# Router rows of layer 0 turned behind the next batch's queries, into a buffer of their own

## Chip, cores and metric

One core of a Trainium2 chip runs the whole program. Its engines are TensorE (PE, with its weight loads as PEld), VectorE (DVE), ScalarE (ACT) and GpSimd (POOL), each with a queue of its own that runs in order; SyncE (SP) issues most transfers. The metric is the device time of one execution in microseconds.

## What is computed

Four batches of 512 rows of width 256 pass through two layers. Cut to the steps in question:

```
x = x + tanh(g) * MLP(attention(layernorm(x), ctx))      # layer 0, 16 heads, 64 context rows
n = layernorm(x)
logits = n @ router_w + router_b                          # 8 experts
x = x + tanh(g) * max_prob * expert[argmax](n)            # one expert per row
x = x + tanh(g) * attention(layernorm(x), ctx)            # layer 1
x = x + tanh(g) * ternary_ffn(layernorm(x))
```

## The kernel before, in words

The order of work on each engine is written out by hand, with semaphores between the engines. No scheduler has a part in it. Layer 0 runs in four batches (0 to 3) of four tiles of 128 rows. The function `attention(l, b, first_batch, last_batch)` exists once for each engine and holds that engine's share of batch `b`. It is software-pipelined: while the attention of batch `b` runs, the normalised rows of batch `b+1` are turned and multiplied to queries, and the router's work for batch `b-1` is done, whose rows were finished at the end of the batch before.

TensorE does this in a batch of layer 0: `turn(0)`, scores of tile 2, `turn(1)`, scores of tile 3 (`turn` transposes the probabilities of one tile into the two PSUM banks `t_bank`, L740; `scores` is L724); then `router_turn(b-1)` (L881), eight transposes of the rows that VectorE's second layer norm wrote (`xn2`, printed as `ew`), which wait for `ln["rt"]["xn"]`; then `values(0)` (L758), between whose halves stand `router_products(b-1)` (L888, sixteen recorded products of 8 columns), the small `weight_sum` (L857) and `turn_rows(b+1)` (L696); then `queries(b+1)` (L711) in two halves, of which the second overwrites a bank in which `weight_sum` and the router left results, and so waits for VectorE's `w_mean` (L1512) and logits (L1534); then `turn(2)`, scores of the next batch's tile 0, `turn(3)`, `values(1)`, and the products of the MLP (L812, then L827).

ScalarE copies what is turned out of `t_bank` to SBUF: `turned` (L1167) for the probabilities, `router_rows` (L1142) for the router's rows, `turned_rows` (L1127) for the query rows. The last two write the same buffer, `xn_t`. Its order in a batch is turned(0), turned(1), router_rows, exponentials of tile 2 (L1137), output (L1172), turned_rows, output, exponentials of tile 3, the two copies of the queries (L1132), turned(2), turned(3). The first half of the queries also waits until VectorE has read the bank that it overwrites (`o_lo`, L1560).

VectorE's order is: scores of tile 2 (maximum L1476, difference L1481), a pass over the ternary weights (L1530), sums of tile 2 (L1490, L1493), `o_lo`, scores of tile 3, `o_lo`, `w_mean`, logits, statistics (L1414), sums of tile 3, scores of the next batch's tile 0, the layer norm of the batch after (`xn`, L1436), two more `o_lo`, sums of tile 0, and so on. GpSimd multiplies the probabilities by the reciprocals (L506), and adds the bias rows (L474).

In batch 3 there are no queries; `ternary_chunk` (L874, copied by L1147) is there in their place, in three pairs around turn(2) and turn(3).

## Time and profile before

| what | value |
|---|---|
| median of 3 runs | 603.48 us (597.16 to 603.55) |
| profiled execution, its time | 595.08 us |
| its span | 592.7 us |
| PE, PEld busy | 499.5 us (84%), 364.4 us (61%) |
| DVE, ACT, POOL busy | 419.2, 294.2, 247.1 us |
| mean granted clock of TensorE | 0.927 of full speed |

The numbers below the medians come from the one profiled execution. Busy time says how much an engine has to do, not what ends last. Within layer 0 that is read from the timeline: the bracket behind a row says how long the engine stood idle before it and which instruction released it. Batch 1 of layer 0 begins with the transposes at 63.09 us, batch 2 at 99.97 and batch 3 at 138.73; the expert stage follows at about 200 us.

### The profile page before, as it was taken

The numbers are of one execution on the slowest core, as the hardware profiler recorded it, in microseconds if no ns is written. First come the engines' busy times: TensorE is split into PE (matmuls) and PEld (weight loads), VectorE is DVE, ScalarE is ACT, GpSimd is POOL, SyncE is SP. The second block draws the span as 40 slices with busy tenths as digits, with TensorE's granted clock in tenths as the row PEclk, the third lists the DMA queues.
The fourth block names the chain that finished last, engine by engine and source line by source line (L and its number), as shares of the span: only waits on it lengthen the run. The fifth ranks groups of instructions, "written<-read, shape, count | busy, mean of one in ns | idle before, by whom it ended". The sixth has DMA issues, their size and how long they took to land.

```text
span 592.7 us, 10230 instructions
## 1 busy us (share of the span) xinstructions
PE 499.5 (84%) x3061; PEld 364.4 (61%) x3069; DVE 419.2 (71%) x809; ACT 294.2 (50%) x521; POOL 247.1 (42%) x314
## 2 busy tenths in 40 slices
PE   7888899896998699899999999944897777649994
PEld 3456658566784278788888888812553544425562
DVE  6598898787546987494756823227979899588992
ACT  1446555362654466483755623203454444427884
POOL 5454263344300311020212110066367878538996
PEclk9989899699698899899999999979599989588999
DMA  7940100100167156555554310022000000000112
GB/s 212 296 147 1 37 0 2 36 0 1 35 215 236 31 161 221 180 178 168 174 178 154 94 35 18 18 81 71 0 1 1 1 1 1 0 0 2 36 35 71
DMA packets 35162, 46.40 MB, mean 78 GB/s; under 512 B 2764, under 2 KB 25304, under 8 KB 35128
## 3 DMA queue, kind: packets, MB, share of 16 engines
q1 hardware_dynamic: 30856, 39.02, 20.4%
q0 software_dynamic: 1680, 4.59, 2.7%
q10 hardware_dynamic: 2592, 2.36, 1.2%
q8 instruction: 18, 0.29, 0.2%
q14 instruction: 16, 0.13, 0.1%
HBM read 38.36 MB, written 7.60 MB: 78 GB/s over the span
## 4 chain that ended last, share of the span: by engine, by line
PE 45%; DVE 28%; POOL 10%; issue 7%; ACT 3%; DMA 2%; SPq 2%; DVEq 1%; POOLq 0%; ACTq 0%
PE s_tile L976 16%; PE bank L997 8%; DVE s_max L1476 4%; DVE p_sum L1490 4%; PE bank L827 3%; DVE probs L1481 3%; PE bank L986 3%; DVE stats L1414 2%; DVE xn L1436 2%; DVE ew L1436 2%; PE bank L711 2%; PE s_tile L1070 2%; POOL probs_t L614 2%; DMA w<-in_L_xattn_W 2%; DVE ew_lo L1746 2%
## 5 line engine op out<-in xcount | busy, mean ns | idle before, releaser
L506 POOL TENSOR_TENSOR probs<-probs,p_rcp 128x1024 f32<-128x1024 f32 x32 | 60.9, 1907 | 94.3 <-DVE p_rcp L1493 94.3
L740 PE MATMUL bank<-ident,probs 128*128 128x128 f32 x256 | 40.4, 309 | 27.0 <-POOL probs L506 25.3
L976 PE MATMUL s_tile<-ew_hi,xs_hi 128*128 128x512 f32 x144 | 59.9, 416 | 3.7 <-DVE ew_lo L1746 2.5
L1167 ACT COPY probs_t<-bank 128x512 f32<-128x512 f32 x64 | 35.0, 588 | 47.1 <-PE bank L740 46.7
L976 PE MATMUL s_tile<-ew_hi,xs_lo 128*128 128x512 f32 x144 | 57.5, 399 | 0.0
L976 PE MATMUL s_tile<-ew_lo,xs_hi 128*128 128x512 f32 x144 | 57.4, 398 | 0.0
L740 PEld LDWEIGHTS bank<-ident,probs 128*128 128x128 f32 x256 | 32.9, 159 | 39.5 <-POOL probs L506 30.1
L564 POOL TENSOR_TENSOR token_now<-token_of,carried 128x1 uint32<-128x1 uint32 x17 | 3.8, 226 | 124.1 <-PE bank L960 124.1
L1764 DVE TENSOR_TENSOR probs_t<-s_tile,probs_t 128x512 f32<-128x512 f32 x36 | 24.8, 689 | 43.1 <-PE s_tile L976 41.7
L1137 ACT ACTIVATE probs<-probs 128x1024 f32<-128x1024 f32 x32 | 33.9, 1058 | 33.8 <-DVE probs L1481 33.7
L1476 DVE TENSOR_REDUCE s_max<-s_tile 128x16 f32<-128x1024 f32 x32 | 38.4, 1199 | 16.6 <-PE s_tile L724 16.5
L1746 DVE TENSOR_TENSOR ew_lo<-ew,ew_hi 128x512 fp32r<-128x512 f32 x64 | 40.4, 686 | 10.3 <-ACT ew_hi L1254 9.4
L1490 DVE TENSOR_REDUCE p_sum<-probs 128x16 f32<-128x1024 f32 x32 | 38.7, 1209 | 6.4 <-ACT probs L1137 6.3
L724 PE MATMUL s_tile<-k_bd,q_t 64*128 64x256 f32 x256 | 40.6, 433 | 3.0 <-ACT q_t L1132 3.0
L997 PE MATMUL bank<-ew_hi,act_hi 128*128 x144 | 42.2, 293 | 0.0
L1481 DVE TENSOR_TENSOR probs<-s_tile,s_max 128x1024 f32<-128x1024 f32 x32 | 39.2, 1225 | 2.0 <-DVE s_max L1476 0.3
L997 PE MATMUL bank<-ew_lo,act_hi 128*128 x144 | 40.5, 282 | 0.0
L997 PE MATMUL bank<-ew_hi,act_lo 128*128 x144 | 40.3, 280 | 0.0
L1254 ACT CAST ew_hi<-ew 128x512 fp32r<-128x512 f32 x64 | 35.5, 619 | 7.5 <-issue 7.5
L1768 DVE TENSOR_TENSOR act_lo<-bank,act_hi 128x512 fp32r<-128x512 f32 x36 | 24.8, 689 | 18.6 <-ACT act_hi L1295 18.6
L1295 ACT CAST act_hi<-bank 128x512 fp32r<-128x512 f32 x36 | 21.2, 588 | 30.4 <-PE bank L986 30.4
L1285 ACT ACTIVATE probs_t<-s_tile 128x512 f32<-128x512 f32 x36 | 21.5, 599 | 28.3 <-PE s_tile L976 24.6
(228 smaller groups left out, 1318.8 us busy)
## 6 DMA issues: line engine op xcount, KB each, us to landing
ew<-in_L_ffn_w SPq DMA_DIRECT2D x32, 512.0 KB, 5.0
ew<-in_L_ffn_w SPq DMA_DIRECT2D x8, 1024.0 KB, 5.7
slots_y<-xn ACTq DMA_DIRECT2D x18, 128.0 KB, 3.9
x_res<-in_x SPq DMA_DIRECT2D x4, 512.0 KB, 6.4
token_rows<-ew SPq DMA_DIRECT2D x4, 512.0 KB, 3.1
out_rows<-x_res SPq DMA_DIRECT2D x3, 512.0 KB, 3.0
w<-in_L_xattn_W SPq DMA_DIRECT2D x2, 512.0 KB, 9.4
ew<-in_L_ffn_w_gate SPq DMA_DIRECT2D x1, 1024.0 KB, 12.9
```

Of the source, the lines that this page charges most:

```text
L506: nc.gpsimd.tensor_tensor(p, p, p_rcp[:, i, :].unsqueeze(2).to_broadcast([P, H, M]), ALU.mult).then_inc(s["p_norm"], 1)
L724: last = nc.tensor.matmul(s_bank[i % 2][g][:, GH * M * m:GH * M * m + GH * M], q_t[rows, m, P * i:P * i + P], flat(k_bd[rows, m, bass.ds(n ...
L740: last = nc.tensor.transpose(t_bank[c][:, P * j:P * j + P], probs[:, i % 2, at:at + P], ident[:])
L976: last = nc.tensor.matmul(o[:], x, w, start=(k == 0 and n == 0), stop=(k == DK - 1 and n == 2))
L997: last = nc.tensor.matmul(y_bank[:, D * par:D * par + D], u, w, start=(c == 0 and n == 0), stop=(c == EK - 1 and n == 2))
L1137: nc.scalar.activation(probs[:, i % 2, :], probs[:, i % 2, :], ACT.Exp).then_inc(att[l]["a_exp"], 1)
L1167: last = nc.scalar.copy(flat(probs_t[:, i % 2, 4 * c:4 * c + 4, :]), t_bank[c][:])
L1254: last = nc.scalar.copy(hi, w)
L1476: nc.vector.tensor_reduce(s_max[:, i, :], s_tile[i % 2][:].rearrange("p (h s) -> p h s", h=H), AX, ALU.max).then_inc(s["v_max"], 1)
L1481: nc.vector.tensor_tensor(probs[:, i % 2, :].rearrange("p (h s) -> p h s", h=H), s_tile[i % 2][:].rearrange("p (h s) -> p h s", h=H), s_ma ...
L1490: nc.vector.tensor_reduce(p_sum[:, i, :], probs[:, i % 2, :].rearrange("p (h s) -> p h s", h=H), AX, ALU.add).then_inc(s["v_sum"], 1)
L1746: last = nc.vector.tensor_tensor(lo, w, hi.bitcast(F32), ALU.subtract)
```

## The change

The router's rows of batch `b-1` get a buffer of their own, `xr_t`, laid over the values of layer 1 (`v_blk1`, idle until layer 1's values are written; VectorE clears it again in the last batch, 128x1024). With it ScalarE's copies need not share `xn_t`. TensorE no longer turns the router's rows before `values(0)` but after `queries(b+1)`; scores of the next batch's tile 0 come before `turn(2)` instead of behind it; `turn(2)` now waits for ScalarE's two router copies (`r_e`), and the router's products stand between `turn(2)` and `turn(3)`. VectorE's logits move behind the next batch's scores of tile 0 and ahead of its layer norm. Its differences of tile 0 wait for `turn(2)`. The wait for the logits moves from the second half of the queries to the second half of `values(1)`. Layer 0's batch 0, all of layer 1 and the router's work for batch 3 keep their order.

```diff
+        xr_t = v_blk1[:].rearrange("p b j a -> p (b j a)")[:, 0:DK * N].rearrange("p (k n) -> p k n", k=DK)
 # TensorE, queries:
                     if l == 0 and m == 1 and not start:
                         pe.wait_ge(v_wm, n)
-                        if not first:
-                            pe.wait_ge(r_lg, n - 1)
 # TensorE, values:
+                        if half and k and l == 0 and not first_batch:
+                            pe.wait_ge(r_lg, b)
 # TensorE, between():
-                    if l == 0 and not first_batch:
-                        router_products(b - 1)
 # TensorE, attention:
                 scores(l, b, 3)
-                pe.wait_ge(s["a_pt"], TB * b + 2)
-                if l == 0 and not first_batch:
-                    router_turn(b - 1)
                 values(0)
                 if not last_batch:
                     queries(l, b + 1, first_batch, False)
...
+                if l == 0 and not first_batch:
+                    pe.wait_ge(s["a_pt"], TB * b + 2)
+                    router_turn(b - 1)
+                    if not last_batch:
+                        scores(l, b + 1, 0)
+                    pe.wait_ge(r_e, DK * b)
                 turn(2)
...
-                if not last_batch:
+                if not last_batch and (l == 1 or first_batch):
                     scores(l, b + 1, 0)
+                if l == 0 and not first_batch:
+                    if last_batch:
+                        pe.wait_ge(v_olo, 2 * DK * b + DK)
+                    router_products(b - 1, xr_t)
                 turn(3)
 # ScalarE, attention:
                 turned(1)
-                if l == 0 and not first_batch:
-                    router_rows(b - 1)
                 exps(l, b, 2)
                 output(0, 0)
                 if not last_batch:
-                    if l == 0 and not first_batch:
-                        act.wait_ge(r_l, b)
                     turned_rows(l, b + 1)
...
+                if l == 0 and not first_batch:
+                    if not last_batch:
+                        act.wait_ge(r_l, b - 1)
+                    router_rows(b - 1, xr_t)
                 turned(2)
 # VectorE, scores:
-                if i >= 2:
+                if i >= 2 or follows:
                     dve.wait_ge(s["t_pt"], 2 * g - 2)
 # VectorE, attention:
-                if l == 0 and not first_batch:
-                    router_logits(b - 1)
                 if not last_batch:
                     row_stats(phase, TB * b + 2 * TB)
...
-                    scores(l, b + 1, 0)
+                    scores(l, b + 1, 0, True)
                     if l == 0:
+                        if not first_batch:
+                            router_logits(b - 1)
                         dve.wait_ge(s["t_xt"], DK * b + 2 * DK)
                         norm_apply(phase, b + 3, TB * b + 2 * TB, xn)
+                if l == 0 and last_batch:
+                    router_logits(b - 1)
+                    nc.vector.memset(v_blk1[:], 0.0)
```

TensorE in batch 1, from the scores of tile 3 to `turn(3)`. Before:

```order
L724 MATMUL s_tile<-k_bd,q_t 128x256 x4
L881 MATMUL bank<-ident,ew 128x128 x8
L758 MATMUL bank<-probs_t,v_blk 32x256 x4
L888 MATMUL bank<-rw,xn_t 128x8 x8
L857 MATMUL bank<-w_sum,ones 128x1
L696 MATMUL bank<-ident,xn 128x128 x8
L758 MATMUL bank<-probs_t,v_blk 32x256 x4
L711 MATMUL bank<-xn_t,wq 128x512 x4
L740 MATMUL bank<-ident,probs 128x128 x8
L724 MATMUL s_tile<-k_bd,q_t 128x256 x4
L740 MATMUL bank<-ident,probs 128x128 x8
```

and changed (line numbers shift by one to five; `v_blk` is where the router's rows now lie):

```order
L723 MATMUL s_tile<-k_bd,q_t 128x256 x4
L759 MATMUL bank<-probs_t,v_blk 32x256 x4
L862 MATMUL bank<-w_sum,ones 128x1
L697 MATMUL bank<-ident,xn 128x128 x8
L759 MATMUL bank<-probs_t,v_blk 32x256 x4
L710 MATMUL bank<-xn_t,wq 128x512 x4
L886 MATMUL bank<-ident,ew 128x128 x8
L723 MATMUL s_tile<-k_bd,q_t 128x256 x4
L739 MATMUL bank<-ident,probs 128x128 x8
L893 MATMUL bank<-rw,v_blk 128x8 x8
L739 MATMUL bank<-ident,probs 128x128 x8
```

The router's transposes moved behind the queries, the next batch's scores ahead of `turn(2)`, and the router's products from ahead of the queries to directly before `turn(3)`.

TensorE in batch 3, from the scores of tile 3 to the last weight transposes. Before:

```order
L724 MATMUL s_tile<-k_bd,q_t 128x256 x4
L881 MATMUL bank<-ident,ew 128x128 x8
L758 MATMUL bank<-probs_t,v_blk 32x256 x4
L888 MATMUL bank<-rw,xn_t 128x8 x8
L758 MATMUL bank<-probs_t,v_blk 32x256 x4
L874 MATMUL s_tile<-ident_b,ew 128x128 x16
L740 MATMUL bank<-ident,probs 128x128 x8
L874 MATMUL s_tile<-ident_b,ew 128x128 x16
L740 MATMUL bank<-ident,probs 128x128 x8
L874 MATMUL s_tile<-ident_b,ew 128x128 x16
```

and changed:

```order
L723 MATMUL s_tile<-k_bd,q_t 128x256 x4
L759 MATMUL bank<-probs_t,v_blk 32x256 x8
L879 MATMUL s_tile<-ident_b,ew 128x128 x16
L886 MATMUL bank<-ident,ew 128x128 x8
L739 MATMUL bank<-ident,probs 128x128 x8
L879 MATMUL s_tile<-ident_b,ew 128x128 x16
L893 MATMUL bank<-rw,v_blk 128x8 x8
L739 MATMUL bank<-ident,probs 128x128 x8
L879 MATMUL s_tile<-ident_b,ew 128x128 x16
```

The router's transposes now stand between the first weight transposes (the L874, now L879, rows) and `turn(2)`, the products between the second ones and `turn(3)`.

VectorE in batches 1 and 2, around the logits (`w_mean` is the ternary scale, ISA and REGISTER_ALU rows are waits and addresses). Before:

```order
L1560 TENSOR_TENSOR o_lo<-bank,o_hi 128x256
L1511 REGISTER_ALU
L1512 REGISTER_ALU
L1512 TENSOR_SCALAR w_mean<-bank 128x1
L1515 REGISTER_ALU
L1515 RECIPROCAL w_inv<-w_mean 128x1
L1534 ISA
L1534 TENSOR_TENSOR logits<-bank,rb 128x32
L1414 ISA
L1414 BN_STATS stats<-x_res 128x6
```

and changed:

```order
L1480 ISA
L1481 TENSOR_REDUCE s_max<-s_tile 128x16
L1485 ISA
L1486 TENSOR_TENSOR probs<-s_tile,s_max 128x1024
L1539 ISA
L1539 TENSOR_TENSOR logits<-bank,rb 128x32
L1607 ISA
L1441 TENSOR_SCALAR xn<-x_res,mv,rstd 128x256 x4
L1565 TENSOR_TENSOR o_lo<-bank,o_hi 128x256 x2
```

The logits (L1539, before L1534) stood ahead of the statistics; they now stand between the differences and the layer norm `xn`, and wait there for the products.

## Rows read from the trace of the kernel before

**Rows 1.** Table of stretches: start:end, length, busy us (count) of PE, PEld, DVE, ACT, POOL, granted clock, DMA

```profile
69.70:80.30 10.60, 10.37 (x58) 6.40 (x59) 10.10 (x17) 5.45 (x9) 3.77 (x2) 0.85 0.15 51
106.60:120.10 13.50, 13.44 (x58) 8.98 (x59) 10.95 (x18) 5.68 (x9) 3.77 (x2) 0.62 0.12 40
147.30:163.20 15.90, 14.39 (x120) 11.30 (x120) 9.29 (x12) 10.00 (x15) 5.63 (x3) 0.68 0.10 34
```

**Rows 2.** Timeline, TensorE, batch 1: start, duration, line, operation, count, [idle before, releaser]

```profile
69.76 1.94 PE L881 MATMUL bank<-ident,ew 128*128 128x128 f32 x8 [2.42 <-DVE ew L1436]
...
72.64 2.06 PE L888 MATMUL bank<-rw,xn_t 128*128 128x8 f32 x16
...
76.58 3.95 PE L711 MATMUL bank<-xn_t,wq 128*128 128x512 f32 x8 [0.16 <-ACT xn_t L1127]
80.37 1.04 PE L740 MATMUL bank<-ident,probs 128*128 128x128 f32 x8
81.33 1.14 PE L724 MATMUL s_tile<-k_bd,q_t 64*128 64x256 f32 x8
83.28 1.09 PE L740 MATMUL bank<-ident,probs 128*128 128x128 f32 x8 [0.81 <-POOL probs L506]
```

**Rows 3.** Timeline, TensorE's weight loads, batch 1, second half of the queries

```profile
78.55 0.30 PEld L711 LDWEIGHTS bank<-xn_t,wq 128*128 128x128 f32 x2 [0.81 <-DVE w_mean L1512]
```

**Rows 4.** Timeline, VectorE, batch 1

```profile
74.74 0.37 DVE L1560 TENSOR_TENSOR o_lo<-bank,o_hi 128x256 fp32r<-128x256 f32 x1
...
77.85 0.15 DVE L1512 TENSOR_SCALAR w_mean<-bank 128x1 f32 x1
...
78.28 0.19 DVE L1534 TENSOR_TENSOR logits<-bank,rb 128x32 f32 x1
...
82.52 1.22 DVE L1476 TENSOR_REDUCE s_max<-s_tile 128x16 f32<-128x1024 f32 x1 [0.98 <-PE s_tile L724]
...
84.92 3.01 DVE L1436 TENSOR_SCALAR xn<-x_res,mv,rstd 128x256 f32 x4
...
88.50 1.21 DVE L1490 TENSOR_REDUCE p_sum<-probs 128x16 f32<-128x1024 f32 x1
```

**Rows 5.** Timeline, ScalarE, batch 1

```profile
72.22 1.06 ACT L1137 ACTIVATE probs<-probs 128x1024 f32<-128x1024 f32 x1
...
75.45 1.07 ACT L1127 COPY xn_t<-bank 128x512 f32<-128x512 f32 x2 [1.91 <-PE bank L696]
...
80.57 0.69 ACT L1132 ACTIVATE q_t<-bank,bq_s 128x512 f32<-128x512 f32 x1 [1.28 <-PE bank L711]
...
86.50 1.06 ACT L1137 ACTIVATE probs<-probs 128x1024 f32<-128x1024 f32 x1
```

**Rows 6.** Timeline, TensorE, batch 2

```profile
106.66 1.60 PE L881 MATMUL bank<-ident,ew 128*128 128x128 f32 x8 [2.45 <-DVE ew L1436]
...
109.20 3.58 PE L888 MATMUL bank<-rw,xn_t 128*128 128x8 f32 x16
...
122.27 1.09 PE L740 MATMUL bank<-ident,probs 128*128 128x128 f32 x8
```

**Rows 7.** Timeline, VectorE, batch 2

```profile
116.50 0.42 DVE L1560 TENSOR_TENSOR o_lo<-bank,o_hi 128x256 fp32r<-128x256 f32 x1 [2.08 <-ACT o_hi L1172]
```

**Rows 8.** Timeline, all engines, batch 3, in order of start

```profile
147.34 1.33 PE L881 MATMUL bank<-ident,ew 128*128 128x128 f32 x8 [4.36 <-DVE ew L1436]
...
151.88 1.22 DVE L1481 TENSOR_TENSOR probs<-s_tile,s_max 128x1024 f32<-128x1024 f32 x1
...
155.50 1.92 ACT L1147 COPY gate_t<-s_tile 128x1024 bf16<-128x1024 bf16 x2
...
156.56 1.89 PE L740 MATMUL bank<-ident,probs 128*128 128x128 f32 x8 [0.53 <-POOL probs L506]
...
160.28 1.09 PE L740 MATMUL bank<-ident,probs 128*128 128x128 f32 x8 [0.95 <-POOL probs L506]
```

More of the change, by code:

```diff
@@ L797, in attention @@
                     ternary_chunk(5)
-                    pe.wait_ge(r_lg, B - 1)
                 values(1)
@@ L882, in router_turn, with router_products @@
                     last.then_inc(r_t, 1)
-            def router_products(b):
+            def router_products(b, rows):
                 pe.wait_ge(r_e, DK * b + DK)
@@ L887, in router_products @@
                     for k in range(DK):
-                        last = nc.tensor.matmul(logit_out[:, E * i:E * i + E], xn_t[:, k, P * i:P * i + P],
+                        last = nc.tensor.matmul(logit_out[:, E * i:E * i + E], rows[:, k, P * i:P * i + P],
                                                 rw[:, k, :], start=(k == 0), stop=(k == DK - 1))
@@ L928, in _ @@
             router_turn(B - 1)
-            router_products(B - 1)
+            router_products(B - 1, xn_t)
             pe.wait_ge(r_hot, 1)
@@ L1137, in exps, with router_rows @@
                 nc.scalar.activation(probs[:, i % 2, :], probs[:, i % 2, :], ACT.Exp).then_inc(att[l]["a_exp"], 1)
-            def router_rows(b):
+            def router_rows(b, rows):
                 for k in range(DK):
                     act.wait_ge(r_t, DK * b + k + 1)
-                    nc.scalar.copy(xn_t[:, k, :], t_bank[k][:]).then_inc(r_e, 1)
+                    nc.scalar.copy(rows[:, k, :], t_bank[k][:]).then_inc(r_e, 1)
             def ternary_chunk(n):
@@ L1244, in _ @@
             attention(0, B - 1, False, True)
-            router_rows(B - 1)
+            router_rows(B - 1, xn_t)
             act.wait_ge(r_v, 2)
@@ L1470, in spread_values, with scores @@
                         ALU.add).then_inc(v_vbd, 1)
-            def scores(l, n, i):
+            def scores(l, n, i, follows=False):
                 s = att[l]
```

## The prediction

> **What bounds the kernel now.** I read the table of stretches first, then the timelines of the engines one by one for batches 1, 2 and 3 of layer 0, since the change touches nothing else. In all three batches TensorE finishes the scores of tile 3 and then stands idle for VectorE's second layer norm, whose rows the router's transposes need: 2.42 us in batch 1, 2.45 in batch 2 and 4.36 in batch 3 [rows 2, 6, 8]. That is the wait the change takes away. But the stretch behind it is not TensorE's alone. In batch 1 VectorE is busy for 10.10 of the next 10.60 us [rows 1]; its chain from the layer norm through tile 2, tile 3 and `w_mean` at 77.85 [rows 4] makes TensorE wait again before the second half of the queries, 0.81 us [rows 3], and once more, through GpSimd, before turn(3) [rows 2]. In batch 2 VectorE has a pause of 2.08 us before the second `o_lo` [rows 7], so there TensorE is the one that is late. In batch 3 turn(3) waits for GpSimd [rows 8].
>
> The clock explains the difference. The granted share is 0.85 over 10.60 us in batch 1, 0.62 over 13.50 in batch 2 and 0.68 over 15.90 in batch 3 [rows 1]. With two levels, full (2.4 GHz) and half (1.2), that is 0.15 x 2 x 10.6 = 3.2 us at half clock, then 10.3 and 10.2 us. Each began at the idle stretch. The router's products take 2.06 us in batch 1 and 3.58 in batch 2 [rows 2, 6].
>
> **The wait that goes, and what is late next.** The scores of tile 3 end about 67.3 in batch 1 (69.76 less 2.42). TensorE can now do values(0), the small sum and the query rows' transposes at once, some 2.3 us, until 69.6. Then the queries need two things. ScalarE's copies of the query rows stand behind the exponentials of tile 2 in its queue, which start at 72.22 and take 1.06; with one output and two copies of 1.07 together they are ready at about 74.7 [rows 5]. And the first half overwrites a bank that VectorE reads in `o_lo`, 74.74 plus 0.37 = 75.1 [rows 4]. So a pause of 2.42 becomes one of 5.5 us, and the queries start at 75.1 in place of 76.58 [rows 2]. Of the 1.5 us won here, the second half can use only 0.5: `w_mean` at 77.85 is in VectorE's chain, which starts no earlier than before.
>
> **The clock after that pause.** Rows show half clock after 2.4 us without work, so I take it after 5.5. How long is the open term. The bounds are 0 and 10.3 us; I take 4, nearest to batch 1's 3.2, since in the two long cases the engine spent 3.58 us of it in router products [rows 6], which now come after the queries. The Trainium skill, "TensorE: Matmul & The Clock Gate", section "HAM oscillation — how this bites in real kernels", says that a burst after a long wait starts at the low clock each time and pays for it again; by it the case of zero is out, and the sum would go from +0.3 to what follows. The trace agrees: three waits, three falls.
>
> **Batch 1.** Half of the queries takes 1.8 us at full clock (78.55 to 80.37 [rows 2, 3]), 3.6 at half. First half 75.1 to 78.7, `w_mean` no longer holds anything; the second has 0.4 us at half clock, then 1.6: 80.7. Router transposes, eight as in turn(2), 1.0: 81.7. The scores of tile 0, 1.1 [rows 2]: 82.8. ScalarE meanwhile copies the second query half, 0.69, then the router's rows, two copies like the 1.07 ones [rows 5]: from 80.9 to 82.7. turn(2), 1.0: 83.8. The products at full clock, some 1.9: 85.7. turn(3) starts there, not at 83.28: **2.4 us late**. Before, the products ran while VectorE's chain was the longer one; now they stand between two turns for which the rest waits.
>
> Values, ScalarE's two outputs and the exponentials of the next tile 0 follow turn(3) at a fixed distance, 86.50 plus 2.4 = 88.9, ended 90.0; before they ended at 87.6, and the sums that need them began at 88.50, as VectorE had been busy [rows 4, 5]. So 0.9 is slack and **1.5 us** reach the MLP and the end of the batch. VectorE's logits now wait for the products and hold the layer norm `xn` from 84.92 to about 86.0; with its 3.01 [rows 4] and two `o_lo` it ends by 89.8, still under the 90.0: nothing for it. The maximum of tile 0 starts at 82.9 and not 82.52, under the same cover; without it, 0.4. The moved logits instruction, a product of 128x32, 0.19 [rows 4], leaves the chain ahead of the sums, too little to count.
>
> **Batch 2.** VectorE's pause of 2.08 goes, `w_mean` comes at 114.8 instead of 116.84, and the bank is free 2.7 before that, at 112.0. First half to 115.6, second to 117.6, then the same 5.0 us to turn(3): 122.6 against 122.27 [rows 6], +0.3. Less the 0.9 of slack, which was there too: **-0.6 us**.
>
> **Batch 3.** No queries. VectorE's differences of tile 3 end at 153.1, the exponentials at 154.2, ScalarE's two copies of ternary weights (1.92 [rows 8]) at 156.1, the router copies at 157.3. turn(2) waits for them and starts at 157.4, not 156.56; at half clock, as then, it takes 1.9: 159.3. The weight transposes, 1.6 at half clock: 160.9; the products, taken at full clock as TensorE has then worked for 3.5 us, 1.9: 162.8. turn(3) was at 160.28, released by GpSimd [rows 8]: **+2.5 us**. There is no slack: values(1) and the MLP follow. VectorE's clearing of the buffer, 1024 columns, lies in its wait for values(1).
>
> No transfer moves, and neither does anything on GpSimd or SyncE. Layer 1's new wait is met when reached, because turn(2) stands before those scores there.
>
> **Sum.** 1.5 - 0.6 + 2.5 = +3.4 us. Against the profiled execution, 595.08, that is 598.5. The three runs have a median of 603.48, 8.4 above it, so I forecast 603.48 + 3.4 = **606.9 us**. Bounds: with full clock everywhere batch 1 costs 0.6 (second half 78.1 to 79.9), batch 2 gives 1.3, batch 3 costs 1.0: +0.3. With 10 us of half clock after each pause, 5 us are lost in place of 2: batch 1 +4.5, batch 2 +2.4, batch 3 (products 3.58 and turn(3) doubled too) +4.9: +11.8.
>
> **Rivals.**
> *Slow clock to the end* (0.15): the pause, now 5.5 us, leaves TensorE at half clock through the queries, router transposes, turn(2) and products, as it did for 10.3 and 10.2 us in two of three batches [rows 1]. It costs up to +11.8, 615.3; it decides, past the bound of 1%, when the half clock lasts over about 6.5 us in all three. For it: two of three. Against: the products that ran in the long cases come last now. [...]
> *The wait really goes* (0.07): if VectorE's chain did not hold the queries, 2.42 + 2.45 + 4.36 = 9.2 us would go: 594.3. It needs ScalarE's and VectorE's queues to run ahead; VectorE's 10.10 of 10.60 [rows 1] speaks against it.
> *Batch 2's gain pays for the rest* (0.14): full clock from the queries on, turn(3) there up to the 2.08 earlier [rows 7], batch 1 even, batch 3 +1: about -2, 601.5. For it: nothing but queries follow the pause. Against: all three pauses so far brought the clock down.
> *Forecast* (0.64): +1 to +6.
>
> **Numbers.** A measurement of this kernel can tell about 1%, 6 us, from no change: its own runs lie 597.16 to 603.55. The forecast and the middle rival lie within it. Faster 0.07, from the second rival; slower 0.15, from the first; within 0.78. The range reaches from the middle rival with a fast draw of the runs, 600.0, to the slow clock at about two thirds, 612.0.
>
> **What would show it.** In the changed profile: TensorE idle 5 to 6 us before the queries of batches 1 and 2, released by VectorE's `o_lo` or ScalarE's copies; no wait for `w_mean` in batch 1; turn(2) released by ScalarE's router copies; turn(3) right behind the products, with no wait for GpSimd, 22.6 us after batch 1's first transposes (20.2 before). If turn(3) still waits for GpSimd, the products were hidden and the sum is too high. If the products take 3.5 us there, the first rival holds.

## The result and the profile after

| | before | changed |
|---|---|---|
| median | 598.62 us (592.30 to 603.55, 20 runs) | 604.86 us (599.29 to 607.80, 20 runs) |
| ratio, 95% interval | | 1.0123 [1.0098, 1.0148] |
| profiled execution, time and span | 595.08 and 592.7 us | 601.53 and 599.1 us |
| mean granted clock | 0.927 | 0.917 |
| TensorE, VectorE busy | 499.5, 419.2 us | 498.6, 418.8 us |

The changed kernel is slower by 1.2%, with the same busy time on TensorE and VectorE. The ratio is taken over runs within 1.5% of each kernel's fastest, which leaves out 3 of before's 20 runs here and up to 6 of 29 in the sessions below, so ratio and medians can differ by a few tenths of a percent, and I give both.

To see where the time went I measure each batch of layer 0 from VectorE's first `x_res` addition of the batch before to its own first one. The row for batch 3's beginning and the rows at its end, VectorE's timeline of the changed kernel (start, duration, line, operation, output<-inputs, count, [idle before, releaser]):

```profile
137.44 1.27 DVE L1629 SCALAR_TENSOR_TENSOR x_res<-bank,tg,x_res 128x256 f32 x3 [1.09 <-PE bank L832]
```

```profile
164.07 0.91 DVE L1611 MEMSET v_blk<- 128x1024 f32 x1 [0.16 <-issue]
168.63 0.86 DVE L1565 TENSOR_TENSOR o_lo<-bank,o_hi 128x256 fp32r<-128x256 f32 x2 [3.65 <-ACT o_hi L1177]
...
179.29 0.48 DVE L1629 SCALAR_TENSOR_TENSOR x_res<-bank,tg,x_res 128x256 f32<-128x256 f32 x1 [2.55 <-PE bank L832]
```

179.29 less 137.44 is 41.85 us. Done so in both kernels:

| batch | before | changed | difference | forecast |
|---|---|---|---|---|
| 1 | 36.88 | 37.86 | +0.98 | +1.5 |
| 2 | 38.76 | 37.70 | -1.06 | -0.6 |
| 3 | 36.14 | 41.85 | +5.71 | +2.5 |

The sum is +5.6 of the 6.4 us between the spans. Batch 3 is the whole of it.

TensorE in batch 1 of the changed kernel, which answers to [rows 2, 3]:

```profile
74.91 5.82 PE L710 MATMUL bank<-xn_t,wq 128*128 128x512 f32 x8 [5.46 <-DVE o_lo L1565]
80.56 1.04 PE L886 MATMUL bank<-ident,ew 128*128 128x128 f32 x8
...
83.53 1.85 PE L893 MATMUL bank<-rw,v_blk 128*128 128x8 f32 x16
85.23 1.07 PE L739 MATMUL bank<-ident,probs 128*128 128x128 f32 x8
```

The pause is 5.46 us, ended by `o_lo`; the queries start at 74.91, all in one row, with no wait for `w_mean` inside; the router's transposes, the scores, turn(2), products and turn(3) follow without a gap, and GpSimd releases nothing. Batch 2, answering to [rows 6, 7]:

```profile
112.78 5.66 PE L710 MATMUL bank<-xn_t,wq 128*128 128x512 f32 x8 [5.48 <-DVE o_lo L1565]
...
121.23 1.85 PE L893 MATMUL bank<-rw,v_blk 128*128 128x8 f32 x16
122.94 1.07 PE L739 MATMUL bank<-ident,probs 128*128 128x128 f32 x8
```

The products, 3.58 us before, take 1.85. Batch 3, answering to [rows 8]:

```profile
149.37 1.86 PE L879 MATMUL s_tile<-ident_b,ew 128*128 128x128 bf16 x16 [5.75 <-DVE probs L1486]
151.03 1.91 PE L886 MATMUL bank<-ident,ew 128*128 128x128 f32 x8
156.68 1.97 PE L739 MATMUL bank<-ident,probs 128*128 128x128 f32 x8 [3.74 <-ACT v_blk L1147]
...
160.15 3.53 PE L893 MATMUL bank<-rw,v_blk 128*128 128x8 f32 x16
163.53 1.95 PE L739 MATMUL bank<-ident,probs 128*128 128x128 f32 x8
...
167.12 1.47 PE L759 MATMUL bank<-probs_t,v_blk 128*32 128x256 f32 x16
168.52 0.39 PE L817 MATMUL bank<-o_hi,w_hi 128*128 128x256 f32 x1
```

Here nothing recovers. Transposes of 128x128 that take 1.07 at full clock take 1.95, the products 3.53. Two rows of ScalarE show what turn(2) waited 3.74 us for, as forecast: the router's copies behind the copies of ternary weights.

```profile
153.74 1.91 ACT L1152 COPY gate_t<-s_tile 128x1024 bf16<-128x1024 bf16 x2
155.54 1.09 ACT L1147 COPY v_blk<-bank 128x512 f32<-128x512 f32 x2
```

The table of stretches (start:end, length, busy us (count) of PE, PEld, DVE, ACT, POOL, granted clock, DMA) of the changed kernel, to be held against [rows 1]:

```profile
74.90:79.00 4.10, 4.09 (x5) 1.78 (x6) 3.84 (x9) 1.35 (x2) 3.42 (x2) 0.50 0.00 0
79.00:83.00 4.00, 4.00 (x24) 2.42 (x23) 2.29 (x10) 2.04 (x4) 2.10 (x3) 0.97 0.00 0
...
148.00:168.00 20.00, 14.89 (x100) 13.74 (x104) 9.18 (x12) 9.71 (x14) 5.63 (x3) 0.50 0.08 26
168.00:170.00 2.00, 2.00 (x24) 1.59 (x17) 0.85 (x2) 1.71 (x4) 0.00 (x0) 1.00 0.00 0
```

In batch 1 the half clock (0.50) ends some 4 us after the pause; in batch 3 it begins in the first pause, before 148.0, does not end between the two pauses, and lasts through 20 us, to 168.0. In the kernel before it ended at about 158.2, as 0.94 over 2 us is 0.24 us at half (the times of the clock's falls and returns below are worked out in the same way from stretches of 1 or 2 us):

```profile
156.00:158.00 2.00, 1.47 (x8) 1.45 (x8) 1.11 (x2) 1.65 (x3) 2.00 (x2) 0.50 0.00 0
158.00:160.00 2.00, 1.34 (x19) 1.14 (x17) 0.00 (x0) 1.87 (x4) 2.00 (x2) 0.94 0.00 0
```

The MLP began there at:

```profile
163.21 0.39 PE L812 MATMUL bank<-o_hi,w_hi 128*128 128x256 f32 x1
```

From the `x_res` row, turn(3) starts after 26.09 us (163.53 less 137.44) and before after 22.48 (160.28 [rows 8] less 137.80): +3.61. The MLP starts after 31.08 and 25.41: +5.67, all of batch 3's loss. VectorE's logits and the clearing of the buffer end at 165.0, 3.65 us before VectorE has anything else to do, so they cost nothing.

### The profile page after: what moved, and what is told of

Same layout as the page of the kernel before. It is cut to its first block, busy times and chain, and to the rows that moved or that the text cites. A ratio compares the mean times of both kernels' runs of the same rounds, so it can differ in the third digit from the quotient of the medians.

```text
span 599.1 us, 10241 instructions
## 1 busy us (share of the span) xinstructions
PE 498.6 (83%) x3061; PEld 364.8 (61%) x3069; DVE 418.8 (70%) x810; ACT 294.1 (49%) x521; POOL 246.5 (41%) x314
## 4 chain that ended last, share of the span: by engine, by line
PE 49%; DVE 27%; POOL 7%; issue 7%; ACT 4%; DMA 2%; SPq 2%; DVEq 1%; POOLq 0%; ACTq 0%
PE s_tile L981 17%; PE bank L1002 8%; DVE s_max L1481 5%; DVE p_sum L1495 4%; PE bank L710 3%; PE bank L832 3%; DVE probs L1486 3%; PE bank L991 3%; PE s_tile L1075 3%; DVE ew L1441 2%; DVE stats L1419 2%; PE bank L739 2%; DMA w<-in_L_xattn_W 2%; ACT probs L1142 2%; PE s_tile L723 2%
## 5 line engine op out<-in xcount | busy, mean ns | idle before, releaser
L710 PE MATMUL bank<-xn_t,wq 128*128 128x512 f32 x64 | 33.9, 675 | 16.1 <-DVE o_lo L1565 10.9
```

The costliest lines, as they stand in the source:

```text
L710: last = nc.tensor.matmul(x_bank[m][:], wq[l][:, k, m * P:m * P + P], xn_t[:, k, :], start=(k == 0), stop=(k == DK - 1))
```

## Experiments

Theory: the order by itself costs little; batch 3 is slow because its second pause, 3.74 us in front of turn(2), puts off the return of the full clock, and what follows (turn(2), ternary transposes, products, turn(3), values(1)) is on the path. Rival: ScalarE's copies and the products stand in a row between the turns, and that costs at any clock. Batches below are read as above, in us; time differences are of medians within one session.

| kernel | batches 1, 2, 3 | sum | median less before's | ratio, interval |
|---|---|---|---|---|
| before | 36.88, 38.76, 36.14 | 111.8 | | |
| before, again | 38.26, 38.47, 36.19 | 112.9 | +3.0 | 1.0022 [0.9985, 1.0060] |
| changed | 37.86, 37.70, 41.85 | 117.4 | +6.2 | 1.0123 [1.0098, 1.0148] |
| changed, again | 38.17, 37.87, 41.88 | 117.9 | +8.2 | 1.0105 [1.0048, 1.0162] |
| batch 3 as before | 38.12, 37.82, 36.14 | 112.1 | +1.2 | 1.0060 [1.0028, 1.0092] |
| batch 3's pauses filled | 38.28, 37.93, 36.46 | 112.7 | -1.6 | 1.0003 [0.9964, 1.0043] |
| first pause filled only | 38.10, 37.83, 41.88 | 117.8 | +7.9 | 1.0129 [1.0094, 1.0164] |
| all pauses filled | 37.40, 37.40, 36.48 | 111.3 | -1.4 | 0.9993 [0.9964, 1.0021] |
| products behind turn(3) | 38.27, 37.94, 37.87 | 114.1 | +8.3 | 1.0154 [1.0106, 1.0202] |
| products twice | 43.01, 39.19, 45.90 | 128.1 | +14.0 | 1.0285 [1.0235, 1.0335] |
| before, a pause filled | 36.81, 36.66, 36.82 | 110.3 | -2.2 | 0.9999 [0.9959, 1.0039] |
| router in the pause | 36.49, 36.46, 36.14 | 109.1 | -1.9 | 1.0005 [0.9970, 1.0039] |
| same, short pauses filled | 38.77, 39.60, 36.37 | 114.7 | +3.5 | 1.0098 [1.0059, 1.0136] |
| router in the pause, batch 3 filled | 36.48, 36.48, 36.18 | 109.1 | -2.4 | 0.9941 [0.9907, 0.9974] |

**1. Both kernels again.** No edit. The changed kernel:

> The changed kernel once more, unaltered, for a second profile. Three later profiles had a different first 30 us (granted clock 0.83 there in place of 1.00, and the first x_res row 4 us later), so the profile in which batch 3 took 41.85 us may be one case of several. Theory 'half clock in batch 3 belongs to the changed order': the router's products, the fourth turn, the last ternary transposes and the second values product are at half clock again, batch 3 takes 39.5 us or more from first x_res row to first x_res row (the version with the products behind the fourth turn had the clock back at 161.4 us and took 37.87), and the median is 5 to 7 us over before. Rival 'it was that profile': batch 3 takes 36 to 38 us here, and the loss must be looked for elsewhere.

```profile
160.80 1.97 PE L739 MATMUL bank<-ident,probs 128*128 128x128 f32 x8 [3.74 <-ACT v_blk L1147]
...
164.27 3.53 PE L893 MATMUL bank<-rw,v_blk 128*128 128x8 f32 x16
167.65 1.95 PE L739 MATMUL bank<-ident,probs 128*128 128x128 f32 x8
```

The kernel before:

> The kernel before once more, for a second profile and as a measure of how far two profiles of the same program differ. Expected: ratio 0.997 to 1.003; first x_res row to first x_res row 36.5 to 39 us in batches 1 and 2 (one of them with products of 3.58 us), and batch 3 36 to 37 us whatever the first 30 us are like. If batch 3 took 39 us or more here, its half clock in the changed kernel would not be the change's.

```profile
155.45 3.58 PE L888 MATMUL bank<-rw,xn_t 128*128 128x8 f32 x16
...
165.51 1.10 PE L740 MATMUL bank<-ident,probs 128*128 128x128 f32 x8 [0.65 <-POOL probs L506]
```

Both profiles began otherwise, with a granted clock of 0.83 over the first 30 us in place of 1.00 and the first `x_res` row at 65.5 and 66.3 us in place of 61.9 and 62.2. Batch 3 came out the same to 0.05 us in both kernels: +5.69 again. Batch 1 of before did not: 38.26 for 36.88, with router products of 3.58 us in place of 2.06 and the full clock back 11.7 us after the pause in place of 3.1. So of my three terms that of batch 1 depends on the profile (+0.98, then -0.09), batch 2's is -1.06 and -0.60, batch 3's is fixed. The unchanged kernel's median came out 3.0 us over itself in one session, which is what a median here is worth; the changed kernel's, +8.2 from four runs, is above the 5 to 7 us that I expected.

**2. Batch 3 in the order of before.** Batches 1 and 2 stay changed.

```diff
+                if l == 0 and last_batch:
+                    pe.wait_ge(s["a_pt"], TB * b + 2)
+                    router_turn(b - 1)
                 values(0)
...
-                if l == 0 and not first_batch:
+                if l == 0 and not first_batch and not last_batch:
                     pe.wait_ge(s["a_pt"], TB * b + 2)
                     router_turn(b - 1)
...
```

The products, ScalarE's copies and VectorE's logits of batch 3 go back in the same way.

> The last batch of the first layer (batch 3) runs in the order of the kernel before (router's transposes ahead of the first values product, router products inside it, logits behind the weights' scale); batches 1 and 2 keep the changed order and the buffer of their own. Theory 'batch 3's half clock': the changed kernel's batch 3 took 40.9 us from its start to its first x_res row where the kernel before took 35.2, while batches 1 and 2 together came out at -0.1 us (+0.98 and -1.06). So batch 3 must fall back to about 35.2 us and the time to that of the kernel before, -1 to +1.5 us (ratio 0.998 to 1.003). Rival 'the cost sits in every batch' (the two wins and losses of batches 1 and 2 are a draw by luck of one profile): the time stays 2.5 us or more above before (ratio 1.004 or more).

```profile
149.76 3.58 PE L895 MATMUL bank<-rw,v_blk 128*128 128x8 f32 x16
...
160.44 1.10 PE L739 MATMUL bank<-ident,probs 128*128 128x128 f32 x8 [0.95 <-POOL probs L507]
```

Batch 3 is back at 36.14 and the rows are those of [rows 8], moved by 0.15 us. This puts the loss in batch 3. By its medians the kernel is at +1.2, as expected; its ratio, 1.0060, is above what I gave the theory (1.003) and inside what I gave the rival (1.004 or more), and the sum of the batches, +0.3, does not explain it. Between 0.3 and 3.6 us of the loss may then lie outside batch 3; that stays open.

**3. The two pauses of batch 3 filled.** The order is that of the change.

```diff
                 if l == 0 and last_batch:
+                    keep_running(20, t_bank[0])
                     ternary_chunk(0)
...
                     router_turn(b - 1)
+                    if last_batch:
+                        pe.wait_ge(s["v_sub"], NT)
+                        keep_running(16, s_bank[1][0])
```

> The changed kernel, with products into unused banks in batch 3's two pauses: 20 of 512 columns ahead of the first ternary transposes and 16 behind the router's transposes. Nothing else moves. Theory 'half clock': the granted clock stays at 1.0 there, 16 router products take about 1.9 us in place of 3.53, the turn of the last probabilities and the ternary transposes about half of 1.9 us each, and batch 3 takes 36 to 37.5 us where the changed kernel took 40.9; the time falls by 3 to 5 us against the changed kernel, to +2 to +4 us over before (ratio 1.003 to 1.007). Rival 'the order of the queues': the copies of router rows, the turn behind them and the products in front of the last turn stand in a row whatever the clock; batch 3 stays at 40 us or more and the ratio at 1.010 to 1.014.

```profile
157.01 1.09 PE L739 MATMUL bank<-ident,probs 128*128 128x128 f32 x8 [0.25 <-ACT v_blk L1151]
...
158.83 1.90 PE L897 MATMUL bank<-rw,v_blk 128*128 128x8 f32 x16
160.59 1.07 PE L739 MATMUL bank<-ident,probs 128*128 128x128 f32 x8
```

The stretch that holds them, at full clock (1.00):

```profile
150.00:163.50 13.50, 11.75 (x119) 8.66 (x116) 7.51 (x11) 9.31 (x15) 5.64 (x3) 1.00 0.01 1
```

This decides. turn(2) starts at 157.01, no earlier than in the changed kernel (156.68); the copies, the products and their places are the same. Only the clock differs: products 1.90 and not 3.53, turn(3) 1.07 and not 1.95. The MLP is reached 5 us sooner and batch 3 takes 36.46, so 5.4 of the 5.7 us are the clock and 0.3 is the order. The sum of the batches falls by 4.7, as expected (3 to 5); the medians, each less before's, by 7.8, more than that, and the ratio, 1.0003, is below my 1.003 to 1.007, so the time bears out the direction and not the size.

**4. Only the first pause filled.** As above, without the 16 products in the second.

> The changed kernel with dummy products in the first pause of batch 3 alone (20 of 512 columns, ahead of the first ternary transposes); the second pause, of 3.7 us behind the router's transposes, stays empty. It tells which pause brings the half clock. If it is the first (the ternary transposes behind it already took 1.86 us in place of 1.05), batch 3 takes 36.5 to 37.5 us as with both filled, and the ratio is that of that version (0.998 to 1.004). If the second does it as well, the clock falls during or behind it, the products and the fourth turn are slow all the same, and batch 3 takes 38 us or more, ratio 1.006 or more.

```profile
154.15 1.04 PE L887 MATMUL bank<-ident,ew 128*128 128x128 f32 x8
160.57 1.97 PE L739 MATMUL bank<-ident,probs 128*128 128x128 f32 x8 [5.38 <-ACT v_blk L1148]
...
164.04 3.53 PE L894 MATMUL bank<-rw,v_blk 128*128 128x8 f32 x16
```

The router's transposes before the second pause are at full clock (1.04), turn(2) behind it at half (1.97); the clock fell at 158.3, inside the pause. Batch 3 takes 41.88, as with none filled. So the second pause, which the change made, is enough to cost the time. It is 5.38 us here and not 3.74, as TensorE reached it sooner. (The second filled alone was not run, so what the first one adds in the changed kernel is not shown.) The Trainium skill, "TensorE: Matmul & The Clock Gate", section "HAM oscillation — how this bites in real kernels", says that a wait followed by short work throws the clock down again each time; the trace agrees, with a fall in the second wait although the first had been bridged.

**5. All pauses filled**, with 22 more dummy products before the queries of batches 2 and 3:

```diff
                 values(0)
+                if l == 0 and not first_batch and not last_batch:
+                    pe.wait_ge(s["v_sub"], TB * b + 3)
+                    keep_running(22, s_bank[0][0])
```

> The changed kernel with dummy products in all pauses: 22 of 512 columns in front of the queries of batches 2 and 3 (in batches 1 and 2, where PE idled 5.46 and 5.48 us), and those of the last-batch experiment (20 and 16). Queries took 5.65 us there for 3.95 in the kernel before's batch 1. Theory 'clock': the queries fall to about 4 us and batches 1 and 2 from 38.3 and 37.9 (last-batch experiment, first x_res row to first x_res row) to 36.3 to 37; batch 3 stays at 36.5; time -2 to -4 us against the last-batch experiment, so ratio 0.993 to 0.998 to before. Rival: the fourth turn then waits for GpSimd's probabilities and takes it back, batches 1 and 2 at 37.5 or more, ratio 0.999 to 1.002.

```profile
76.17 4.92 PE L649 MATMUL s_tile<-ident_b 128*128 128x512 bf16 x22 [2.46 <-DVE probs L1493]
80.93 3.60 PE L710 MATMUL bank<-xn_t,wq 128*128 128x512 f32 x8
```

The queries fall from 5.82 to 3.60 us, which gives the term that I had to estimate: 2.2 us more at half clock, so 4.4 us of it after the pause (I took 4). But the dummies end at 80.9, and the queries could have started 5.46 us after the values' end at 73.7, at 79.2: 1.7 us sooner. So only 0.9 and 0.5 us are won of the 2.2. The rival's numbers (37.5 for the batches, 0.999 to 1.002 for the ratio) are nearer, for another reason than it gave.

**6. Products behind turn(3).**

```diff
+                turn(3)
                 if l == 0 and not first_batch:
                     ...
                     router_products(b - 1, xr_t)
-                turn(3)
```

> The changed kernel with the 16 router products behind the fourth turn in place of between the third and the fourth (and the logits behind the normalisation on VectorE). Theory 'clock': the order there is worth little; in batches 1 and 2 PE has no idle time between 82 and 92 us of the changed kernel, so at most 0 to -1 us each; batch 3 stays at half clock and at 40 to 42 us, where the products now lie beside the ACT copies that the second values product waits for, -1 to 0; time -2 to +0.5 us against the changed kernel (ratio to before 1.008 to 1.013). Rival 'products in front of the fourth turn are the cost': batch 3 falls by 3.5 us, batches 1 and 2 by 1.85 each, ratio 1.000 to 1.004.

```profile
158.08 1.97 PE L739 MATMUL bank<-ident,probs 128*128 128x128 f32 x8 [3.74 <-ACT v_blk L1147]
...
161.36 1.06 PE L739 MATMUL bank<-ident,probs 128*128 128x128 f32 x8
```

Batches 1 and 2 are unchanged, as expected; turn(3) stands sooner in the order but waits 0.82 us for ScalarE's copies of the probabilities. In batch 3 of this profile turn(2) started at 158.08, at half clock, and the clock was back at 161.1, before turn(3) and ahead of all work that the edit moves; the batch took 37.87. In the changed kernel the clock had stayed at half from 147.5 to 168.0; here it was back at 154.3, inside the second pause, and fell again at 157.7. So this is not the edit's doing but another case of the same pause, and the profiled run was the shortest of six (600.78 us; four others took 606.73 to 607.84). Four other profiles with that pause left empty (changed, changed again, experiments 4 and 7) had the long case. In time the edit shows no gain: the ratio is 1.0154, over the 1.008 to 1.013 that I expected.

**7. Products twice.**

```diff
-                for i in range(TB):
+                for i in [*range(TB)] * times:
```

> The changed kernel with the router products between the third and fourth turn run twice in each of batches 1 to 3 (the second time with the same result). It prices them where they stand. Theory 'on the path': +1.85 us in each of batches 1 and 2 (16 products of 1.85 us in all at full clock), and +3.5 us in batch 3, where they run at half clock; +7 us against the changed kernel, or +5.5 if the longer busy stretch brings the full clock back sooner in batch 3 (ratio to before 1.021 to 1.025). Rival 'hidden': the fourth turn waits for the normalised probabilities, or the values product for the copies, whatever the products take; 0 to +2 us (ratio 1.012 to 1.016).

```profile
170.48 6.94 PE L893 MATMUL bank<-rw,v_blk 128*128 128x8 f32 x32
```

Against the changed kernel's second profile, which began alike, batch 2 is 1.3 us longer and batch 3 4.0 (products 6.94 for 3.53): they are on the path in both, though batch 2 paid less than the 1.85 expected. Batch 1, 4.8 longer, was a surprise, and with it the ratio, 1.0285 for an expected 1.021 to 1.025:

```profile
87.79 3.99 PE L893 MATMUL bank<-rw,v_blk 128*128 128x8 f32 x32
```

```profile
90.00:92.00 2.00, 2.00 (x15) 2.00 (x15) 0.06 (x1) 0.00 (x0) 0.00 (x0) 0.73 0.00 0
92.00:94.00 2.00, 2.00 (x10) 1.67 (x10) 1.51 (x5) 0.98 (x2) 0.00 (x0) 0.50 0.00 0
```

The clock fell at about 91 us. TensorE had not been idle since 78.60; it had run router products of 8 columns for 3 us. In batch 3 the clock came back 16.0 us after the second pause, at 183.1, for 11.3 in the changed kernel: so the half clock there does not hang on the pause alone, and the longer run of 8-column products went with a later return.

**8. The kernel before, with one pause filled.**

```diff
                 if l == 0 and not first_batch:
+                    keep_running(16 if last_batch else 9, t_bank[0])
                     router_turn(b - 1)
```

> The kernel before, with products of 512 columns into an unused bank in the pause ahead of the router's transposes: 9 in batches 1 and 2, 16 in batch 3. It tells how much of the kernel before is half clock too, so what the change could have won or lost by it. From first x_res row to first x_res row, batches 1, 2 and 3 took 36.88, 38.76 and 36.14 us before. Theory 'the clock decides in every batch': batch 2 (products 3.58 us, queries slow) falls to 36.5 to 37 us, batch 3 (products 3.53 us, values and transposes slow) to 33 to 34.5, batch 1 stays at 36.5 to 37 because the fourth turn waits for GpSimd there; time -3 to -5 us against before (ratio 0.992 to 0.995). Rival 'the waits on GpSimd and VectorE take it back': batch 3 at 35.5 or more and batch 2 at 38 or more, ratio 0.998 to 1.002.

```profile
150.51 1.95 PE L889 MATMUL bank<-rw,xn_t 128*128 128x8 f32 x16 [0.16 <-ACT xn_t L1143]
...
158.00 1.97 PE L740 MATMUL bank<-ident,probs 128*128 128x128 f32 x8 [3.15 <-POOL probs L506]
```

Batch 2 falls to 36.66, as the theory had it: 2.1 us of its 38.76 were half clock, of which the change took out 1.06. Batch 3 does not fall (36.82): products at 1.95 and not 3.58 only lead to a wait of 3.15 us for GpSimd's probabilities. In the order of before the half clock of batch 3 was free, covered by GpSimd (part of this batch still ran at half clock, from 152.9 to 163.2; experiment 11 has it all at full). My number for batch 3 (33 to 34.5) was wrong and the rival right there, as it was on the ratio, 0.9999 for my 0.992 to 0.995.

**9. The router's work in the pause.** The buffer used another way: in batches 1 and 2 the next batch's rows are turned and copied first, then the router's transposes, copies and products, all ahead of values(0)'s second half; batch 3 as before.

```diff
                     if not last_batch:
                         turn_rows(l, b + 1)
+                    if l == 0 and not first_batch:
+                        if not last_batch:
+                            pe.wait_ge(s["a_xt"], DK * b + 2 * DK)
+                            router_turn(b - 1)
+                        router_products(b - 1, xr_t)
```

> The buffer of its own, used another way: in batches 1 and 2 the next batch's rows are turned and copied first, the router's transposes, copies and products follow inside the same pause ahead of the queries' second half; nothing of the router stands between the third and fourth turn any more, and batch 3 is in the order of before. Theory 'the pause is the right place': batch 3 at 35 to 36 us; batches 1 and 2 keep PE busy in the pause in which it idled 5.5 us in the changed kernel, and their later part loses 2.8 us of transposes and products; time 0 to -3 us against before (ratio 0.995 to 1.000). Rival: queries wait for the logits as in the kernel before, and the copies of router rows now delay them on top; then batches 1 and 2 are each up to 1.9 us longer than before, ratio up to 1.006.

```profile
73.88 1.10 PE L885 MATMUL bank<-ident,ew 128*128 128x128 f32 x8 [0.73 <-ACT xn_t L1131]
75.71 1.95 PE L892 MATMUL bank<-rw,v_blk 128*128 128x8 f32 x16 [0.73 <-ACT v_blk L1146]
...
79.19 6.45 PE L712 MATMUL bank<-xn_t,wq 128*128 128x512 f32 x8 [0.82 <-DVE o_lo L1565]
```

One pause of 5.46 has become three of 0.73, 0.73 and 0.82 with the router's work between them. The batches sum to 109.1, 2.7 under before, median -1.9; the ratio, 1.0005, does not tell it from no change. The queries still take 6.45 us: half clock again, though no pause ahead of them is longer than 0.82 us.

**10. The same with its short pauses filled.**

```diff
                         if not last_batch:
+                            pe.wait_ge(s["v_sub"], TB * b + 3)
+                            keep_running(3, s_bank[0][0])
                             pe.wait_ge(s["a_xt"], DK * b + 2 * DK)
                             router_turn(b - 1)
+                            keep_running(3, s_bank[0][0])
...
```

> The version with the router's work inside the pause (batches 36.49, 36.46 and 36.14 us), its pauses filled: 3 dummy products of 512 columns in each of three short pauses in batches 1 and 2 (0.73, 0.73 and 0.82 us), 16 ahead of the router's transposes in batch 3 (4.36 us). Queries took 6.45 and 5.27 us there. Theory 'clock': queries about 4 us, batches 1 and 2 at 35 to 36 us with the fourth turn waiting for GpSimd, batch 3 at 33.5 to 34.5; sum 104 to 106 us against 111.8 before; the time 4 to 7 us under before (ratio 0.988 to 0.994), the fastest of all. Rival: the gain of the clock is taken back by waits for GpSimd and VectorE, sum 108 or more, ratio 0.995 to 1.000.

```profile
75.71 0.82 PE L649 MATMUL s_tile<-ident_b 128*128 128x512 bf16 x3 [3.03 <-DVE probs L1492]
```

A miss of mine: the bank for the dummies is free only once VectorE has made the differences of tile 2, so the router's transposes waited 3.03 us where they had waited 0.73. Batches 38.77 and 39.60. It says nothing on the clock.

**11. Router in the pause, batch 3 filled.** Experiment 9, with dummies in batch 3 in two places whose banks are free:

```diff
+                    keep_running(18, t_bank[0])
                     router_turn(b - 1)
...
                     ternary_chunk(1)
+                    pe.wait_ge(s["v_sub"], NT)
+                    keep_running(12, s_bank[1][0])
                 turn(2)
```

> A version meant to beat both: the router's work inside the pause in batches 1 and 2 (36.49 and 36.46 us), batch 3 in the order of before with its two pauses filled (18 dummy products ahead of the router's transposes, 12 behind the first ternary transposes, where the kernel before with only the first filled idled 3.15 us and then went on at half clock for 5.6 us). Theory 'clock': batch 3 at 33.5 to 35 us from first x_res row to first x_res row, sum of the three 106.5 to 108 us against 111.78 before, time 3 to 5 us under before (ratio 0.992 to 0.996). Rival: batch 3 waits for GpSimd's probabilities whatever the clock and stays at 36 us, ratio 0.997 to 1.001.

```profile
154.96 1.09 PE L741 MATMUL bank<-ident,probs 128*128 128x128 f32 x8 [0.63 <-POOL probs L507]
...
158.69 1.09 PE L741 MATMUL bank<-ident,probs 128*128 128x128 f32 x8 [1.75 <-POOL probs L507]
```

```profile
140.00:182.00 42.00, 38.15 (x279) 26.40 (x277) 24.91 (x45) 18.52 (x29) 11.25 (x8) 1.00 0.31 101
```

Batch 3 runs at full clock throughout (1.00) and takes 36.18, to 0.04 us what it took at half clock: turn(2) and turn(3) wait 0.63 and 1.75 for GpSimd. The theory's number for it was wrong, the rival's right. The median is 2.4 us under before and the ratio 0.9941 [0.9907, 0.9974], the one version whose interval lies below 1. The ratio fell where I had it, by luck, as batch 3 gave nothing. Its batches sum to the same as those of experiment 9, whose ratio was 1.0005, so the gain that the traces support is 2.6 us of 111.8, 0.4% of the whole, and that it is real is likely rather than shown.

## Why the prediction was right or wrong

The time, 606.9, is 2.0 over the measured 604.86, inside 600.0 to 612.0. But it stood on a median of 603.48 from three runs; over twenty, before is 598.62. The change itself is +6.2 us by medians and 1.2% by ratio, where I forecast +3.4 and gave 0.15 to more than 1%. The base was 4.9 us too high and the change's size 2.8 too low; that the two nearly cancel is luck.

- **The pause.** Forecast 5.5 us, queries at 75.1; 5.46 and 74.91. Both right, and so was what ends the pause, `o_lo`.
- **Batch 1, +1.5.** turn(3) 22.4 us after the batch's first transposes (forecast 22.6), released by nothing but the products. The batch cost +0.98 in one pair of profiles, -0.09 in the other. The forecast was too high in both; before's batch 1 had a short half clock in the first profile (3.4 us) and a long one in the second (10.2), by luck and not by its order.
- **Batch 2, -0.6.** The two pairs gave -1.06 and -0.60. Right.
- **The length of the half clock after the pause, 4 us.** Experiment 5 gives 4.4 in batch 1 (5.82 less 3.60, twice), and the granted clock itself was back 4.3 and 4.0 us after the pauses of batches 1 and 2. Right for these two, and for the reason given: in seven profiles it came back 2.8 to 5.5 us after each such pause that the queries followed.
- **Batch 3, +2.5.** This is the step that failed, in its words "the products, taken at full clock as TensorE has then worked for 3.5 us, 1.9". They took 3.53, and turn(3), the ternary transposes and values(1) behind them ran at half clock too. The mechanism, copies before turn(2) and products before turn(3), was right: turn(2) came 19.24 us after the `x_res` row, forecast 19.6. The term measured +5.7. Experiment 3 shows that at full clock the same order costs +0.3, less even than my lower bound of 1.0. I had sized one unknown, the length of the half clock, from batch 1 and used it in batch 3, though both long cases of [rows 1] spoke for 10 us: before, the last real pause ended at 147.34 and the clock returned at 158.2, 10.9 us later; changed, the last pause ended at 156.68 and it returned at 168.0, 11.3 later. The change moved batch 3's last long pause back by 9.3 us and with it the return of the clock. The reason for 4 us, that queries come first and products last, did not hold in batch 3, which has no queries. My upper bound for batch 3, +4.9, had this case, and was 0.8 short, as the ternary transposes and values(1) were slow too.
- **No slack in batch 3.** Right for the changed order and wrong for the old one: before, 10 us of half clock cost nothing, as the turns waited for GpSimd (experiments 8 and 11). That cover is what the change removed.
- **Rivals.** At +6.2 by medians the change lies just above the +1 to +6 of *Forecast*, at +5.6 by the batches inside it. *Slow clock to the end* was true of batch 3 and false of 1 and 2; a rival by batch, and not for all three at once, would have held the result. *The wait really goes* was rightly small: the pause grew to 5.46. *Batch 2's gain pays for the rest* needed batch 3 at +1, which experiment 3 gives (+0.3) only with the pauses filled.

Open: whether the 0.6% of experiment 2 is real, and where; what made the clock return early in the one profile of experiment 6 and in batch 1 of before's first; and how much of the 11 us is owed to the pause and how much to the 8-column products behind it, which no run took out of batch 3 with the pause left in (the last section has the cases that speak for the products).

## What to carry over

Put the engine's own small work into its pauses and not behind them, and before moving work out of a pause ask what clock the rest then runs at: here half clock around two pauses of 5.75 and 3.74 us cost 5.4 us in work that was on the path, while 10 us of half clock had been free where another engine was the later one. The first half of this rests on experiment 9's batches (2.7 us shorter), not on its time, which does not differ from before's. Size such an unknown for each stretch from stretches with the same work behind the pause, and from more than one profile: the same pause in batch 1 of before had 3.4 us of half clock once and 10.2 the next time. Dummy products help only where they end before the real work could start, and where the bank they write is free; with the wrong wait in front they cost more than they save (experiments 5 and 10).

## What the runs showed of the hardware

- How soon the full clock came back depended on what followed the pause. Where the queries of 512 columns followed a pause of 5.5 us, it took 2.8 to 5.5 us (14 pauses in seven profiles). Where transposes of 128 columns, values products and router products of 8 columns followed a pause of 2.4 to 5.4 us, it took 10.6 to 11.7 us in ten of thirteen, although TensorE was busy nearly all that time, 16.0 us with the router products doubled (experiment 7), and 3.1 us in two (batch 1 of before, batch 3 of experiment 6). In these two it was back before the router products or as they began (at 72.9 in before, where they start at 72.64), and in batch 3 of experiments 8 and 10, where they stand ahead of the pause, it was back 5.2 and 3.5 us behind it.
- The clock also fell without any pause, at about 91 us in experiment 7, after 3 us of 8-column products behind 9 us of other work, and with no pause over 1 us in batches 1 and 2 of experiments 9 and 11.
- The first 30 us, the same work in all kernels, ran at a mean granted clock of 1.00 or 0.83 from one execution to the next (6 and 8 of the 14 profiles), and the first `x_res` row moved by about 4 us with it.
- VectorE's four `xn` instructions in batch 1 took 3.01 us where they ran beside GpSimd's `x_res` addition for 1.88 us (before [rows 4], that addition at 84.44 to 86.80), 1.73 beside 0.62 (experiment 9), 1.65 beside 0.53 (changed) and 1.38 beside 0.2 (both second profiles).
